# Row-tiled scores and row maxima from packed keys, with two heads' maxima emptied by one VectorE instruction

## The reference, cut to what matters

```
scores = einsum('bhsk,bhtk->bhst', Q, K) / sqrt(width)
attn   = softmax(scores, axis=-1)
ao     = einsum('bhst,bhtv->bhsv', attn, V)
```

## Time and profile before

| | |
|---|---|
| median of 3 runs | 543.95 us (543.36 to 544.02) |
| span of the profiled execution | 541.2 us, 7612 instructions |
| around the span (median less span) | 2.75 us |
| PE busy | 494.7 us (91%) |
| DVE busy | 315.8 us (58%) |
| ACT busy | 278.7 us (51%) |
| POOL busy | 136.3 us (25%) |
| mean granted TensorE clock | 0.978 |

### The profile page before, as it was taken

One profiled execution on the slowest core, in us unless ns is written; L12 is line 12 of the kernel. 1 busy time (PEld: TensorE's weight loads), 2 busy tenths in 40 slices (PEclk: granted clock), 3 DMA queues, 4 the chain that ended last, 5 costly groups with the idle time before them and its releaser, 6 DMA issues.

```text
span 541.2 us, 7612 instructions
## 1 busy us (share of the span) xinstructions
PE 494.7 (91%) x2782; PEld 345.1 (64%) x2782; DVE 315.8 (58%) x826; ACT 278.7 (51%) x414; POOL 136.3 (25%) x136
## 2 busy tenths in 40 slices
PE   5899799998989999999999988999999999889980
PEld 4578678886545555554897865445555554669970
DVE  4654444567778787764263577877788663402223
ACT  6734344552546566667454653556656555205640
POOL 5755622331711101200000000101111005231551
PEclk9999899999999999999999998999999999899995
DMA  8970200000700000020000000000000002540003
GB/s 323 303 234 2 78 1 0 1 1 1 307 5 0 1 2 0 1 79 0 2 1 0 1 2 1 1 0 1 0 1 2 0 1 94 249 107 4 19 18 120
DMA packets 12868, 26.57 MB, mean 49 GB/s; under 512 B 1293, under 2 KB 10120, under 8 KB 11808
## 3 DMA queue, kind: packets, MB, share of 16 engines
q1 hardware_dynamic: 11392, 22.91, 12.5%
q0 software_dynamic: 1440, 3.18, 1.9%
HBM read 22.11 MB, written 5.26 MB: 51 GB/s over the span
## 4 chain that ended last, share of the span: by engine, by line
PE 77%; DVE 10%; ACT 5%; issue 3%; DMA 3%; POOL 2%; POOLq 0%; DVEq 0%; SPq 0%; ACTq 0%
PE PS L436 13%; PE PS L468 11%; PE PS L453 10%; PE PS L690 5%; PE PS L579 5%; PE PS L613 5%; PE PS L581 5%; PE PS L580 5%; PE PS L730 3%; PE PS L721 3%; DVE mx L1153 3%; PE PS L342 3%; PE PS L421 2%; PE PS L422 1%; PE PS L443 1%
## 5 line engine op out<-in xcount | busy, mean ns | idle before, releaser
L1153 DVE TENSOR_REDUCE mx<-PS 128x1 f32<-128x512 f32 x256 | 164.6, 685 | 41.8 <-PE PS L436 39.3
L854 ACT ACTIVATE wc_late<-PS 128x1024 f32<-128x1024 f32 x128 | 123.9, 1022 | 62.2 <-PE PS L453 62.0
L436 PE MATMUL PS<-Kp,Qs 128*128 128x512 f32 x256 | 95.9, 438 | 6.9 <-DVE mx L1153 5.2
L436 PEld LDWEIGHTS PS<-Kp,Qs 128*128 128x128 f32 x256 | 44.7, 190 | 70.4 <-DVE mx L1153 40.3
L453 PE MATMUL PS<-Qm,Kp 128*128 128x512 f32 x256 | 75.2, 415 | 0.8 <-DVE Qm L1165 0.6
L468 PE MATMUL PS<-wc_late,v_c 128*16 128x512 f32 x512 | 67.3, 598 | 0.7 <-ACT wc_late L854 0.7
L1438 POOL CAST Kp<-Ks 32x512 fp32r<-32x512 f32 x40 | 24.3, 607 | 135.0 <-ACT Ks L833 133.1
L453 PEld LDWEIGHTS PS<-Qm,Kp 128*128 128x128 f32 x256 | 46.5, 190 | 18.1 <-ACT wc_late L854 3.8
L579 PE MATMUL PS<-wc_late_r 128*128 128x512 f32 x96 | 41.7, 435 | 1.1 <-POOL xT_yT_r L1400 0.6
L1052 DVE TENSOR_SCALAR work<-PS,early 128x512 f32<-128x512 f32 x32 | 22.6, 747 | 25.1 <-PE PS L581 25.1
L954 ACT ACTIVATE work<-PS,late 128x160 f32<-128x160 f32 x64 | 19.8, 396 | 32.5 <-PE PS L721 32.5
(11 more groups left out here) (244 smaller groups left out, 743.5 us busy)
## 6 DMA issues: line engine op xcount, KB each, us to landing
wa<-wa_dram SPq DMA_DIRECT2D x8, 512.0 KB, 9.0
wa<-wc_dram SPq DMA_DIRECT2D x2, 2048.0 KB, 9.8
wc_late<-wc_dram SPq DMA_DIRECT2D x2, 2048.0 KB, 11.1
wb<-wb_dram SPq DMA_DIRECT2D x1, 2048.0 KB, 15.6
sel<-sel_dram POOLq DMA_DIRECT2D x2, 1024.0 KB, 5.6
late<-late_dram SPq DMA_DIRECT2D x1, 1572.0 KB, 14.9
packed_rows<-ao SPq DMA_DIRECT2D x1, 1290.0 KB, 22.9
wb<-packed_rows SPq DMA_DIRECT2D x5, 258.0 KB, 4.3
```

The source lines that it names most:

```text
L436: filled(mm(p, Qs[:, G % 3, qt * P:(qt + 1) * P], Kp[:, G % 3, j, :], start=True, stop=True), (L, "max", G, qt, j))
L854: A(E4[:, 2 * (i % 2) + jp, :, :], p, ACT.Exp, scale=float(HD[L]) ** -0.5).then_inc(taken[f"s{jp}"], 1)
L1153: V.reduce_max(mx[:, G % 2, qt, j:j + 1], p, AX.X).then_inc(taken[filled_at[key][0]], 1)
```

## The change

Keys are kept packed: Ks has three buffers of 128x512, and Kp, its memset, ACT's four pieces (now one instruction for each group, for all groups) and the placing on POOL go. Each head's matmul reads only its own 32 partitions of Ks and Qs or Qm, at the row position of these partitions. In the loops the maxima of two heads go into one slot mm, made of the two banks of m0 and m1, and one `reduce_max` of 128x1024 empties it into two columns. The early halves before the loops stay as two matmuls in two slots and two reductions, but they read the packed keys too.

```diff
-        Kp = sb("Kp", [P, 3, HPG, S], F32R)
-        Ks = sb("Ks", [P, 2, S])
+        Ks = sb("Ks", [P, 3, S], F32R)
...
-        SLOTS = {"m0": (0, 1), "m1": (1, 2), "s0": (2, 4), "s1": (4, 6), "pv": (6, 7), "mi": (7, 8)}
+        SLOTS = {"m0": (0, 1), "m1": (1, 2), "mm": (0, 2), "s0": (2, 4), "s1": (4, 6), "pv": (6, 7), "mi": (7, 8)}
...
                 if fills[s]:
                     pe.wait_ge(taken[s], fills[s])
+                for other in {"mm": ("m0", "m1"), "m0": ("mm",), "m1": ("mm",)}.get(s, ()):
+                    if fills[other]:
+                        pe.wait_ge(taken[other], fills[other])
...
-                    mm(ps("m0"), Qs[:, 0, 0:P], Kp[:, 0, 0, :], start=True, stop=True)
+                    mm(ps("m0"), Qs[:, 0, 0:P], Ks[:, 0, :], start=True, stop=True)
...
-                def maxima(m, half, slots=("m0", "m1")):
+                def maxima(m, half, slots="mm"):
...
-                    if qt == 0 and G >= 3:
-
-                        pe.wait_ge(Kp_set, HPG * (L * KEYS + G - 3) + 2 * (half + 1))
+                    if slots == "mm":
+                        p = claim((L, "max", G, qt, half), "mm")
+                        for j in range(2):
+                            r = slice(SL * (2 * half + j), SL * (2 * half + j + 1))
+                            last = mm(p[:, j, :], Qs[r, G % 3, qt * P:(qt + 1) * P], Ks[r, G % 3, :], start=True,
+                                      stop=True, tile_position=(SL * (2 * half + j), 0))
+                        filled(last, (L, "max", G, qt, half))
+                        return
                     for j in (2 * half, 2 * half + 1):
                         p = claim((L, "max", G, qt, j), slots[j % 2])
-                        filled(mm(p, Qs[:, G % 3, qt * P:(qt + 1) * P], Kp[:, G % 3, j, :], start=True, stop=True),
-                               (L, "max", G, qt, j))
+                        r = slice(SL * j, SL * (j + 1))
+                        filled(mm(p, Qs[r, G % 3, qt * P:(qt + 1) * P], Ks[r, G % 3, :], start=True, stop=True,
+                                  tile_position=(SL * j, 0)), (L, "max", G, qt, j))
...
                     for j in range(2):
-                        last = mm(p[:, j, :], Kp[:, G % 3, 2 * jp + j, kt * P:(kt + 1) * P], Qm[:, G % 2, :],
-                                  start=True, stop=True)
+                        r = slice(SL * (2 * jp + j), SL * (2 * jp + j + 1))
+                        last = mm(p[:, j, :], Ks[r, G % 3, kt * P:(kt + 1) * P], Qm[r, G % 2, :], start=True, stop=True,
+                                  tile_position=(SL * (2 * jp + j), 0))
...
-                def stackK(G, half):
...
+                def stackK(G):
                     p = wait_full(act, (L, "stack", G, 0))
-                    for j in (2 * half, 2 * half + 1):
-                        r = slice(SL * j, SL * (j + 1))
-                        last = A(Kp[r, G % 3, j, :], p[r, :], ACT.Identity, bias=la("minus")[r, :])
-                    if half:
-                        last.then_inc(taken["mi"], 1)
+                    A(Ks[:, G % 3, :], p, ACT.Identity, bias=la("minus")).then_inc(taken["mi"], 1)
...
+                    if filled_at[L, "max", G, qt, half][0] == "mm":
+                        key = (L, "max", G, qt, half)
+                        p = wait_full(dve, key)
+                        V.reduce_max(mx[:, G % 2, qt, 2 * half:2 * half + 2], p, AX.X).then_inc(taken["mm"], 1)
+                        return
...
-            nc.gpsimd.memset(Kp[:, :, :, :].rearrange("p a j s -> p (a j s)").bitcast(F32), 0.0)
...
-            def place_keys(L):
...
-            place_keys(0)
...
-            place_keys(1)
```

More of the change, by code:

```diff
@@ L265, in jobs @@
             if place == 0:
-                return {0: [("stackK2", G + 2)] * (more and G > 0), 1: [("stackQ", G + 2)] * more,
-                        2: [("turn", G - 1)] * (G > 0),
+                return {0: [], 1: [("stackQ", G + 2)] * more, 2: [("turn", G - 1)] * (G > 0),
                         3: [("maxT", G + 1)] * (G + 1 < NGB)}[kt]
@@ L283, in build @@
         early_jobs = [{(8, 1): [("cT", 0)], (9, 0): [("qk", 0, 0)], (9, 1): [("v", 0)],
-                       (10, 0): [("stackK", 0), ("stackK2", 0)], (10, 1): [("stackQ", 0)],
-                       (12, 1): [("stackK", 1), ("stackK2", 1)], (13, 1): [("stackQ", 1)],
-                       (14, 1): [("stackK", 2), ("stackK2", 2), ("place", 0)],
+                       (10, 0): [("stackK", 0)], (10, 1): [("stackQ", 0)],
+                       (12, 1): [("stackK", 1)], (13, 1): [("stackQ", 1)],
+                       (14, 1): [("stackK", 2), ("place", 0)],
                        (15, 0): [("maxT", 0), ("max", TPB, 0)], (15, 1): [("max", TPB, 1)]},
                       {(8, 0): [("cT", 0)], (8, 1): [("qk", 0, 0)], (9, 0): [("qk", 0, 1)],
-                       (9, 1): [("stackK", 0), ("stackK2", 0)], (10, 1): [("stackQ", 0)], (11, 0): [("v", 0)],
-                       (11, 1): [("stackK", 1), ("stackK2", 1)], (12, 1): [("stackQ", 1)], (13, 0): [("tanh", 0)],
-                       (13, 1): [("stackK", 2), ("stackK2", 2)], (14, 1): [("place", 0), ("coh", 0)],
+                       (9, 1): [("stackK", 0)], (10, 1): [("stackQ", 0)], (11, 0): [("v", 0)],
+                       (11, 1): [("stackK", 1)], (12, 1): [("stackQ", 1)], (13, 0): [("tanh", 0)],
+                       (13, 1): [("stackK", 2)], (14, 1): [("place", 0), ("coh", 0)],
                        (15, 0): [("maxT", 0), ("max", TPB, 0)], (15, 1): [("max", TPB, 1)]}]
@@ L349, in keep_warm @@
                 pe.wait_ge(taken["m0"], fills["m0"])
+                pe.wait_ge(taken["mm"], fills["mm"])
                 for _ in range(n):
-                    mm(ps("m0"), Qs[:, 0, 0:P], Kp[:, 0, 0, :], start=True, stop=True)
+                    mm(ps("m0"), Qs[:, 0, 0:P], Ks[:, 0, :], start=True, stop=True)
             def field(step):
@@ L534, in job @@
                         maxima(*at)
-                    elif name not in ("stackK2", "place"):
+                    elif name != "place":
                         {"y": y_, "logits": logits, "count": count, "weightsT": lambda b: weightsT("b", b),
@@ L883, in job @@
                 def job(name, *at):
-                    if name in ("stackK", "stackK2"):
-                        stackK(at[0], int(name == "stackK2"))
+                    if name == "stackK":
+                        stackK(*at)
                     elif name in ("cT", "qk", "tanh", "coh", "stackQ", "aoT", "proj", "logits", "count"):
@@ L1157, in place @@
                         dve.wait_ge(clear0, 1)
-                    for j in (HPG - 2, HPG - 1):
-                        wait_taken(dve, (L, "max", G, TPB - 1, j))
+                    if G < 1:
+                        for j in (HPG - 2, HPG - 1):
+                            wait_taken(dve, (L, "max", G, TPB - 1, j))
+                    else:
+                        wait_taken(dve, (L, "max", G, TPB - 1, 1))
                     link(V.tensor_copy(MP[:, :, :, 0], mx[:, G % 2, :, :]))
@@ L1430, in part_mla @@
                 nc.gpsimd.tensor_tensor(mla_low[:, m], mlaT[:, m], mla_high[:, m], ALU.subtract).then_inc(mla_split, 1)
-            def place_keys(L):
-                for G in range(3, NGB):
-                    wait_taken(pool, (L, "stack", G, 0))
-                    for j in range(HPG):
-                        rows = slice(SL * j, SL * (j + 1))
-                        nc.gpsimd.tensor_copy(Kp[rows, G % 3, j, :], Ks[rows, G % 2, :]).then_inc(Kp_set, 1)
-                        pool.wait_ge(Kp_set, HPG * (L * KEYS + G - 3) + j + 1)
             pool.wait_ge(wb_split, EB)
-            place_keys(0)
             part_mla(0)
```

10 lines of the change are left out of this document (1 added, 9 removed).

## The result

The changed kernel takes 591.0 us (median of 4 runs, 580.86 to 597.58) against 543.99 us: a ratio of 1.0743, 95% interval 1.0656 to 1.0830. The kernel after spreads over 3% and its mean clock is 0.852 to 0.889 in all four runs, where the kernel before has 0.978; the ratio is that of the two faster runs (580.86 and 589.42), so the change costs some 40 us by it and 47 by the medians. Every run lies above the prediction's range (542 to 573) and above the forecast's own (549 to 566).

A forecast was written before the change was run, and what follows sets the result against it. Loops bound by a chain passing between TensorE and VectorE. Loops +8.0 and +4.6, last steps -2, early halves +2, keys -0.5: +12.1, rounded up to +13 on 543.95, so 557 us; range 542 to 573.

The forecast's parts named there:

- Reduction of 128x1024: VectorE's single maxima reduction per pair in the loops: predicted 1.22 us, with bounds of 1.13 and 1.37.
- Fill: Time from a pair's first maxima weight load until both heads' matmuls fill the slot: taken as 0.62 us.
- The rival that the tiles don't run at once: Row-tiled maxima run one after the other: fill 0.77, a pair 2.04, 571 us in all; chance 0.09.
- A pair at least 1.89: In the loops, fill 0.62, reduction 1.22 and 0.05 to the next weight load take turns: 1.89 us a pair.
- The sum for the loops, +12.6 us: Predicted growth of both attention loops: first +8.0 us (107.4 against 99.4), second +4.6 us (110.2 against 105.6).
- Mode changes: Full-array jobs between row-tiled maxima and column-tiled values drain PE: 0.53 us from maxima to job load; 6.3 us a loop.
- Scores' weight loads 0.11 apart: Four row-tiled scores take some 0.45 us instead of 1.00 until the next load; VectorE's loop hides the gain.
- Early halves, +2: 20 pairs inside the expert stages get two mode changes each: at most +2.8 us, taken as +2.
- VectorE's other work at nothing: Place, normalisation and Qm fit VectorE's 0.67 us wait per pair, costing nothing; uncovered, some 1.7 us in each group.
- Keys, POOL and memset near nothing: Dropping ACT's early key instructions gains 0.5 us; dropping POOL's 24.3 us of casts and a memset gains 0.
- the clock at no cost in the forecast: PE's clock in the loops was taken to stay at full speed, with its fall priced only as a rival.
- The rival's price: PE idling lowers the clock for a quarter of the loops, 2.3 us a step: +30, 587 us; chance 0.05.

The follow-up runs named there:

- two fillers: The changed kernel with two extra full-array 128x512 matmuls before the scores of each step: 570.64 us, ratio 1.0510 to the kernel before.

## Why the prediction was wrong

By its own steps:

- **Reduction of 128x1024**, taken as 1.22: 1.224. Right, worked out from another operation's price for a column.
- **Fill**, taken as 0.62: 0.54 at full clock (204.22 to 204.76), the low bound. The Trainium skill (TensorE: Matmul & The Clock Gate, part 3) has row tiles of one set starting about 4 ns apart; the estimate of 0.54 worked out from it agrees with this trace's 0.54. The rival that the tiles don't run at once is out.
- **A pair at least 1.89**: pairs at full clock without a job are 1.82 (202.94 to 204.76 between reductions), and 1.98 on average in the longest stretch at full clock. The sum for the loops, +12.6 us, stands beside some +5 us that one stretch gives. For full-array matmuls the same working is too cheap: with a fill of 0.77 a pair is 2.05, some 12 us over the loops of before, and in the run with the slot alone the loops (140.85 to 253.08 and 346.49 to 462.05) took 22.8 us more, 2.15 a pair. What makes up the rest stays open. That row tiles at full clock pay for most of the slot is read from the changed kernel's stretches and not from a run of its own.
- **Mode changes**: a maxima LD is followed by the job's after 0.42 (204.22 to 204.64) and not 0.13. I had 0.53. Right in kind, a little too dear.
- **Scores' weight loads 0.11 apart**: the two of one slot start together, and all four take 0.19 us in the run with row-tiled scores alone. Too dear, but in a half where VectorE hides it.
- **Early halves, +2**: the first loop starts later by no more than the start of the kernel explains, and between the loops the time grew by 0.2 us. Nothing of it shows.
- **VectorE's other work at nothing**: VectorE waits 0.5 to 0.9 us in front of most reductions at full clock, and Qm and the normalisation lie in such waits. Nothing speaks against it.
- **Keys, POOL and memset near nothing**: nothing in the rows speaks against it; it wasn't tried alone.
- **The step that failed: the clock at no cost in the forecast.** I took the granted clock to stay at 1.00, priced its fall as a rival with 5%, and argued from the busy share ("the step would still be some three quarters busy"). The busy share was indeed 83%, and that argument is the error: with PE busy for 4.00 of 4.00 us the clock was 0.50 when only 32 rows worked. So the fall came from the 32-row matmuls and at most in part from the idling that the rival gave as its reason. The rival's price (587 us, a quarter of the loops at half clock, 2.3 us a step) was near in time by luck: 54% of the loops ran slow (134 of 249 us), at 1.1 us a step in the stretches compared (2.54 against 1.98 a pair) and 1.5 by the averages (2.7 against 1.94).

What the clock and the turn-taking take: with two fillers the loops' share of slow clock fell and some 13 us went although work was added, so the clock takes at least some 13 of the 40 us (by the ratios). From the pairs of the one profiled execution it is about 39 of 43.9 us in the loops. The single slot alone costs 24 us with full-array matmuls, and leaving it out of the change gives 17 back. The two counts don't contradict each other: the slot also lengthens the time at half clock (134 us in the loops with it, 78 without). So the parts don't add up one by one, and a version of the change at full clock throughout wasn't reached.

## What to carry to other kernels

Here row-tiled matmuls paid where all four row positions work at once (the scores, -1.1%) and not where two of four do (the maxima, +4.3%, mode changes included). Read the granted clock and not the busy share of PE before and after. A PSUM slot that one instruction fills and empties as a whole turns two engines from overlapping to taking turns: price the pair as fill plus drain before counting the saved instruction, here 0.07 us against 0.54 to 0.77. And where an engine waits for another, quicker work beside it can go into the wait: the quicker scores turned one wait of 0.35 us into two of 0.43 and 0.41.

## What the hardware showed that I had not expected

- 32-row matmuls of 512 columns, always at the same row position, kept PE busy 100% with the clock at 0.50 (1.2 GHz) in windows of 16 us together, while full-array matmuls of the same product had 1.00; 960 of them on four positions at once kept it at 1.00 (2.4 GHz) for 54.7 us.
- Four weight loads at different row positions take 0.19 us together, as one full-array load takes; two full-array ones take 0.30.
- Full-array matmuls whose weight loads wait 0.82 us in each 2.05 us (PE busy 89 to 90%) did not lower the clock (0.98 and 1.00 over the loops).
- Moving a job of 0.75 us into what looked like a wait of 0.35 us cost 1.4%.
